# Expert up-projections with the weights stationary, in a mixture-of-experts kernel on one core

## The reference

```python
probs = jax.nn.softmax(x @ wg.T, axis=-1)
topk_w, topk_idx = jax.lax.top_k(probs, 2)
topk_w = topk_w / jnp.sum(topk_w, axis=-1, keepdims=True)
expert_w = jnp.sum(jax.nn.one_hot(topk_idx, E) * topk_w[..., None], axis=1)
h1 = jnp.einsum('th,eih->tei', x, w1)      # w1, w3: (8, 512, 256)
h3 = jnp.einsum('th,eih->tei', x, w3)
y = jnp.einsum('tei,ehi->teh', jax.nn.silu(h1) * h3, w2)
out = jnp.einsum('te,teh->th', expert_w, y)
```

## Time and profile before

| | |
|---|---|
| runs of the kernel | 529.51 us median of 3 (527.03 to 531.07) |
| the profiled execution | 527.7 us, its span 525.2 us |
| TensorE busy | 497.2 us of the span (95%) |
| VectorE, ScalarE, GpSimd busy | 377.1, 286.5, 277.9 us |
| first ups of the experts (tile 0) | at 335.78 us |
| ups of the last tile (tile 38) | at 503.78 us |

### The profile page before, as it was taken

One profiled execution on the slowest core, in us unless ns is written; L12 is line 12 of the kernel. 1 busy time (PEld: TensorE's weight loads), 2 busy tenths in 40 slices (PEclk: granted clock), 3 DMA queues, 4 the chain that ended last, 5 costly groups with the idle time before them and its releaser, 6 DMA issues.

```text
span 525.2 us, 10993 instructions
## 1 busy us (share of the span) xinstructions
PE 497.2 (95%) x3686; PEld 326.1 (62%) x3686; DVE 377.1 (72%) x978; ACT 286.5 (55%) x575; POOL 277.9 (53%) x312
## 2 busy tenths in 40 slices
PE   7899999999999999999999999999999899999990
PEld 3576766656566666666666766655566555566660
DVE  6899887588878668968988999987878334344440
ACT  4556867647467745764649558654553333344420
POOL 4463213003643609993595862555755656776663
PEclk9999999999999999999999999999999999999995
DMA  8012534246887537884599680366696666788973
GB/s 278 14 32 71 170 101 116 86 103 105 149 177 123 150 78 166 141 163 154 109 198 192 126 277 2 91 122 109 103 205 99 111 119 120 124 136 120 129 89 39
DMA packets 135313, 65.60 MB, mean 125 GB/s; under 512 B 109757, under 2 KB 126590, under 8 KB 135262
## 3 DMA queue, kind: packets, MB, share of 16 engines
q1 hardware_dynamic: 127774, 54.69, 48.9%
q0 software_dynamic: 7488, 10.23, 12.0%
HBM read 28.19 MB, written 10.35 MB: 73 GB/s over the span
## 4 chain that ended last, share of the span: by engine, by line
PE 49%; issue 12%; DVE 12%; DMA 11%; ACT 7%; POOL 6%; POOLq 2%; SPq 1%; DVEq 0%; ACTq 0%
PE ps L1205 38%; DMA out<-y,qst 7%; POOL y L942 3%; DMA probT<-prob 3%; PE ps L1300 3%; PE ps L1302 3%; PE ps L1301 3%; ACT ps L1016 2%; DVE cmax L1744 2%; POOLq L962 2%; POOL out L968 2%; ACT tT L1002 1%; ACT prob L1015 1%; DVE ps L2335 1%; DMA stage<-we_in 1%
## 5 line engine op out<-in xcount | busy, mean ns | idle before, releaser
L1205 PE MATMUL ps<-arena,probT 128*128 128x256 f16 (+2 forms) x1092 | 180.7, 318 | 5.6 <-ACT probT L1002 2.4
L1205 PEld LDWEIGHTS ps<-arena,probT 128*128 128x128 f16 (+1 forms) x1092 | 104.4, 97 | 63.7 <-issue 12.4
L968 POOL DMA_INDIRECT out<-y,qst x39 | 63.2, 1620 | 14.1 <-issue 7.8
L1205 PE MATMUL ps<-arena,qT 128*128 128x512 f16 (+1 forms) x384 | 69.1, 332 | 1.0 <-DVE prob L1885 0.7
L1015 ACT ACTIVATE prob<-ps,nbias 128x512 f16<-128x512 f32 x64 | 39.0, 609 | 50.4 <-DVE nbias L1750 50.4
L1143 ACT ACTIVATE w1m<-ps 128x512 f32<-128x512 f32 x39 | 23.3, 598 | 75.5 <-PE ps L1205 65.1
L1205 PE MATMUL ps<-arena,tT 128*128 x468 | 57.2, 273 | 0.6 <-DVE tT L2442 0.6
L791 POOL TENSOR_TENSOR rstd<-veps,expo 128x1 f32<-128x1 f32 x16 | 9.0, 560 | 91.3 <-DVE veps L1779 91.3
L2335 DVE SCALAR_TENSOR_TENSOR ps<-ps,w1m 128x512 f32<-128x512 f32 x39 | 27.2, 697 | 39.1 <-ACT w1m L1143 33.7
L1205 PEld LDWEIGHTS ps<-arena,qT 128*128 128x128 f16 x384 | 32.5, 97 | 36.0 <-issue 1.7
L942 POOL DMA_INDIRECT y<-hrow,qst x39 | 40.4, 1035 | 24.3 <-DVE qst L2107 13.4
(11 more groups left out here) (240 smaller groups left out, 907.1 us busy)
## 6 DMA issues: line engine op xcount, KB each, us to landing
stage<-we_in SPq DMA_DIRECT2D x33, 256.0 KB, 3.0
prob<-we_in SPq DMA_DIRECT2D x15, 256.0 KB, 4.4
xin<-x_in SPq DMA_DIRECT2D x16, 128.0 KB, 2.7
out<-y SPq DMA_DIRECT2D x16, 128.0 KB
hrow<-tT SPq DMA_DIRECT2D x4, 512.0 KB
y<-x_in SPq DMA_DIRECT2D x3, 512.0 KB, 6.9
stage<-z_in SPq DMA_DIRECT2D x4, 256.0 KB, 5.3
prob<-w_in SPq DMA_DIRECT2D x4, 256.0 KB, 3.1
```

Of the source, the lines that this page charges most:

```text
L968: g.indirect_dma_start(out[:rows_of(p), :], bass.IndirectOffsetOnAxis(ridx[:, n:n + 1], 0), ys[:, n % RING, :], None, compute_op=ALU.add). ...
L1205: r = t.matmul(o, lhs(a), rhs(b), start=first and n == 0, stop=last and n == 2)
```

## The change

The two operands of the up products change places. Before, the tile's turned rows `xT` were stationary and 512 columns of weights moved. Now a 128 x 128 block of the weights is stationary and the 128 columns of `xT` move; the 512 result rows of one product are made as four blocks of 128, side by side in the same bank. The result then stands with the hidden index on the partitions and the tokens in the columns, which is the form that the downs need. So `act_hi` and `act_lo` write straight into `actT`, `act_turn` and `last_turn` go, and `e_downs` waits for `e_alo` of its tile. `act_hi` waits for the downs that read its slot before, in place of the DMA transpose. SP's two last stores keep their places by waits for `e_alo`.

```diff
@@ e_ups @@
                 for h in range(2):
-                    for k in range(KD):
-                        r = mm3(ps[2 * q + h][:], lambda a: xT[:, q, a * KD + k, :],
-                                lambda b: ew[:, at + (k * 2 + h), b, :], k == 0, k == KD - 1)
+                    for f in range(KI):
+                        for k in range(KD):
+                            r = mm3(ps[2 * q + h][:, f * P:(f + 1) * P],
+                                    lambda a: ew[:, at + (k * 2 + h), a, f * P:(f + 1) * P],
+                                    lambda b: xT[:, q, b * KD + k, :], k == 0, k == KD - 1)
@@ e_downs @@
-                if n < NJ - 1:
-                    pe.wait_ge(sm[f"e_a{s}"], 4 * (n - s) + 16)
-                else:
-                    wait(pe, "e_lcp", 2)
+                wait(pe, "e_alo", n + 1)
@@ act_hi (ScalarE) @@
-                if not (isinstance(n, int) and n < RING):
-                    act_.wait_ge(sm[f"e_a{s}"], 4 * (n - s))
-                copy(arow[:, s, 0, :], ps[2 * (s % 2) + 1][:]).then_inc(sm["e_ahi"], 1)
+                if n >= RING:
+                    wait(act_, "e_down", n - RING + 1)
+                copy(act_row(s, 0), ps[2 * (s % 2) + 1][:]).then_inc(sm["e_ahi"], 1)
@@ act_lo (VectorE) @@
-                v.tensor_tensor(arow[:, s, 1, :], ps[2 * (s % 2) + 1][:], arow[:, s, 0, :],
+                v.tensor_tensor(act_row(s, 1), ps[2 * (s % 2) + 1][:], act_row(s, 0),
                                 ALU.subtract).then_inc(sm["e_alo"], 1)
@@ SP @@
-            for n in range(NJ):
-                if n < NJ - 1:
-                    act_turn(n)
-                if n == 8:
-                    store_x1(sp, NB - 1, range(NT - TB, NT))
-                if n == H_AT:
-                    store_h(sp, NB - 1)
+            wait(sp, "e_alo", 9)
+            store_x1(sp, NB - 1, range(NT - TB, NT))
+            wait(sp, "e_alo", H_AT + 1)
+            store_h(sp, NB - 1)
@@ the end of TensorE's program @@
             e_downs(NJ - 2, (NJ - 2) % RING)
-            last_turn()
             e_downs(NJ - 1, (NJ - 1) % RING)
```

More of the change, by code:

```diff
@@ L164, in xattn_ffn_moe, with act_row @@
         actT = tT[:, 0:4096].rearrange("p (s a k c) -> p s a k c", s=RING, a=2, k=KI)
-        arow = prob[:, 1, :].bitcast(F16).rearrange("p (s a c) -> p s a c", s=RING, a=2)
+        def act_row(s, a):
+            return actT[:, s, a].rearrange("p k c -> p (k c)")
         xg = y[:, 0:RING, :].bitcast(F16)
@@ L324, in xattn_ffn_moe @@
             h_out x1_out fill_out r_count r_tab r_next r_made r_listed r_list chain links_p
-            e_x0 e_x1 e_x2 e_x3 e_a0 e_a1 e_a2 e_a3 e_xtr e_xcp e_up e_sil e_act e_ahi e_alo e_down e_y
-            e_add0 e_add1 e_add2 e_add3 e_ltr e_lcp""".split()
+            e_x0 e_x1 e_x2 e_x3 e_xtr e_xcp e_up e_sil e_act e_ahi e_alo e_down e_y
+            e_add0 e_add1 e_add2 e_add3""".split()
         sm = {n: sem(n) for n in names}
@@ L577, in list_cols @@
             return bank[:, :3 * (PHASES[p][2] - PHASES[p][1])]
-        def last_bank(a):
-            return ps[2 - 2 * ((NJ - 1) % 2) + a][:].bitcast(F16)[:, :CH]
         def x_bank(n):
@@ L699, in _ @@
                         store_x1(sp, j, range(j * TB + 2 * (i - at), j * TB + 2 * (i - at) + 2))
[L701 to L708, removed]
             loads(chunk_from(2), chunk_from(2) + len(CHUNK_PIECES[2]))
@@ L1192, in _ @@
                 e_step(n, n % RING, n + 1 < NJ)
-            wait(act_, "e_ltr", 1)
-            copy(actT[:, (NJ - 1) % RING, 0].rearrange("p k c -> p (k c)"),
-                 last_bank(0)).then_inc(sm["e_lcp"], 1)
         @block.tensor
@@ L2440, in _ @@
             e_step(NJ - 1, (NJ - 1) % RING, NJ - 3)
-            wait(dve, "e_ltr", 2)
-            v.tensor_copy(actT[:, (NJ - 1) % RING, 1].rearrange("p k c -> p (k c)"),
-                          last_bank(1)).then_inc(sm["e_lcp"], 1)
             weighted(NJ - 2, (NJ - 2) % RING)
```

## The result

| | before | changed |
|---|---|---|
| runs beside each other | 530.29 us median of 4 (527.03 to 531.24) | 596.39 us median of 4 (595.86 to 596.89) |
| the profiled execution, its span | 527.7, 525.2 us | 596.9, 594.7 us |
| ups of tile 3 to ups of tile 38 | 157.2 us | 223.4 us |
| ups of tile 38 to the end | 21.4 us | 18.5 us |

The ratio is 1.126, 95% interval 1.121 to 1.131: the changed kernel is 66 us slower.

A forecast was written before the change was run, and what follows sets the result against it. The prediction took the array, streaming without a gap at 4.12 us a tile, to bound the kernel before. Terms of +67.3, +5.6 and -2 gave +70.9 us, so 600 us on the median; range 585 to 618.

The forecast's parts named there:

- The array: In the ups, 48 matmuls of 128 columns instead of 12 of 512: 2.7 us against 2.6, +0.1 a tile.
- The sequencer: TensorE's ups, main term: 32 register operations at 0.133 us plus 0.65 for the offset load, 4.9 us, nothing hiding it.
- The period: Time per tile, the longer of sequencer (6.1 us) and chain through silu and x_copy (6.26); taken as 6.3 with late loads.
- Late loads: Some offset loads between the halves of the ups take up to 0.98 us instead of 0.31, now exposed: +0.1 in the mean.
- Tiles 0 to 2: The first three tiles, which have no downs: 16.4 us instead of 10.8, +5.6.
- The end: From the ups of tile 38 on: 18.5 to 20.2 us instead of 21.4, taken as -2.
- The DMA transposes: Removing 38 transposes from the DMA side: counted as zero; without the long period at most 3.4 us of TensorE's waits.
- The rival in which the freed DMA engines pay: Register operations hidden, adds land faster, VectorE's and TensorE's waits go: 524.5 us, faster by 1%; chance 3%.
- Hidden register operations: Rival: the sequencer's weight-address operations cost almost nothing or are merged, 526 to 533 us, no change; chance 4%.
- the bound by weight loads: Rival: in the ups, pairs with 128 columns cannot keep 0.057 us; at 0.083, +1.4 a tile, 583 us; chance 4%.
- a dearer weight load with a register address: Rival: in the ups, 0.03 us more on each register operation makes a period of 7.3 and 635 us; chance 9%.
- The granted clock: Rival: the clock granted falls, with the array streaming 4.2 us of 6.3; chance 3%.

The follow-up runs named there:

- fixed addresses: Changed kernel with the ups of every tile reading expert 0's weights at a fixed address: 520.88 us; the same edit in the kernel before: 527.77 us.
- the run that copies tile 0's register: Changed kernel without the offset loads of tiles 1 to 38, each tile's register made from tile 0's, all register operations kept: 573.03 us, ratio 1.082.
- the runs with 24 and 32 operations: Changed kernel with part of the low-half weights read at expert 0's fixed address, 24 register operations in the ups: 562.14 us; unedited, 32: 596.39 us.
- moving the load: Changed kernel with the next expert's offset load moved from between the halves of the ups to ahead of the wait for x_copy: 596.36 us, ratio 1.128.
- the cut alone: Kernel before, rows still stationary and DMA transposes kept, with the 512 moving weight columns cut into four matmuls of 128: 599.7 us, ratio 1.137.
- the early load and ScalarE's order turned: Changed kernel with the offset load ahead of the wait for x_copy and ScalarE's order x_copy(n+1), silu(n), act_hi(n): 599.25 us, ratio 1.133.
- The program whose register doesn't change: Changed kernel in which all tiles use tile 0's register, without 38 of 39 offset loads: 528.53 us, ratio 1.000.

## Why the prediction came out right

**The array** (+0.1 a tile): right, 0.056 a pair with fixed addresses. Before, TensorE was the bound of the stage, busy 95% of the span and 20.00 of 20 us from 470 to 490.

**The sequencer**: right, and by the right price. Before, it made the last address of the downs at 467.8 and the next tile's first at 469.2, behind the end of x_copy at 469.12, and waited some 1.3 us in between. I took 0.133 for an operation and 0.65 for the load. The trace has 16 starts over 2.0 us, and the run that copies tile 0's register gives 0.61 for each. The ups took 4.94 where I had 5.0. The 0.11 of the runs with 24 and 32 operations is less, probably since some of the 0.133 is the issue of the pairs, which stays; no run separates the two. The bounds of 0.125 and 0.14 were well chosen.

**The period** (6.3): measured 6.35 in this tile, 6.25 in the mean from tile 16 to tile 37, and 223.4 us over 35 tiles where I had 224.5. The chain does come last, as I said. But the step that compared the two terms was only half right. I had 6.1 for the sequencer and 6.26 for the chain. Without the chain's share the sequencer alone still holds 6.27. My sum for it was 0.2 short. Half of that are small pauses between the operations (39 steps over 5.4 us are 0.138, the wait ahead of the downs included). The other half is a second wait, for act_lo ahead of the ups, that takes the sequencer 0.1 (475.42 to 475.52 in that trace) and that my sum left out. The two terms are equal. That is why moving the load gained nothing, where I had expected 8 to 16 us in that experiment. A period that is the longer of two nearly equal terms is forecast well by either, and says nothing of what an edit to one of them brings.

**Late loads** (+0.1): didn't come. The longest load went from 981 to 490 ns; in this trace nothing held one up for long.

**Tiles 0 to 2** (+5.6): ups 0 stands at 337.34 and ups 3 at 352.86, 15.5 us where I had 16.4; together with a start 1.6 us later than before it is +6.3.

**The end** (-2): 18.5 us, so -2.9. The last add starts 10.3 us after the ups of tile 38, at the lower bound I gave. It follows the one before without a wait for a landing.

**The DMA transposes** (zero): right for this sum, as the wait for adds was off the path at 6.3 us a tile. The 3.4 us that I allowed for a kernel without that long period were too few for the stage: putting the transposes back lengthens it by 7.8 us, against TensorE's own waits of 2.4 and 1.0 in the earlier trace rows, and the end by 3.4. The rival in which the freed DMA engines pay had the mechanism, and its 3.4 and 4.6 us are near the measured 9.8; the register operations kept it from the time.

**ScalarE's and VectorE's new waits** (zero): right, neither shows a wait for the downs of tile n-4.

**The rivals.** Hidden register operations, the bound by weight loads and a dearer weight load with a register address are refuted by the runs with 24, with fixed addresses, and with the cut alone. The granted clock did not fall: it was 1.00 of full speed from 470 to 490 us, as before; what a fall would cost, no run shows.

The sum came out within 1% without the terms all being right. Late loads (6.3 in place of 6.26, some 1.4 us over the stage) and the first tiles (0.9 us) were put too high, the start of the stage (1.6 us later than before) had no term, and the end gave back 0.9 more than I took. These errors are small beside the main term, which is right by its cause and its price.

No version that beats both kernels was found. The gain of 8 us that fixed addresses show is gone with 16 address operations a tile already (529.28 us). With the weights stationary in blocks of 128 columns, the widest in any of these kernels, the up weights of a tile make 32.

## What to carry to other kernels

Where addresses are made at run time, count them as instructions of the engine's own queue and set them against the time in which the array does the work between them. Making a dynamic operand's pieces four times narrower cost almost nothing in the array here (2.68 against 2.58 us a tile) and four times as many operations in the sequencer. Put a run-time address on the operand that is read in the widest pieces, and look at starts, not at the busy share, to see it.

## What the runs showed of the hardware

- A register operation listed at 46 ns takes 0.123 us (31 steps in 4.04 - 0.22, the ups at 447.60 with the early load and ScalarE's order turned) to 0.138 (39 steps in 5.4, the early load alone) of TensorE's sequencer with its one or two pairs. Once the sequencer is slower than the array, each further one costs 0.11 us (24 against 32 a tile).
- An offset load is listed at 0.30 us, but costs 0.61 (38 loads, 23.4 us): behind it stand a register operation of 151 ns and an assertion of 18 ns on the value's range.
- Pairs of weight load and matmul at 128 columns ran at 0.056 us over 48 in a row, with all addresses fixed.
- The program whose register doesn't change made 40 addresses up to 351.8 us and none again; 1,560 register operations fell to 40.
- When its sequencer feeds it too slowly, TensorE is still shown 88 to 99% busy (17.65 of 20 us in the changed kernel, 79.59 of 80 in the run that copies tile 0's register).
- DMA transposes slowed GpSimd's adds into DRAM: with 38 of them put back, the DMA share rose from 0.42 to 0.77 and VectorE's waits for adds from 7.8 to 34.5 us.
